# An attention and FFN layer on one core: mixing weights by eight indirect DMAs in place of one-hot matmuls

## What is computed

```python
def cond(x, weights, condition):          # weights [16, 32, 32]
    W = weights[condition]                # one 32x32 matrix for each batch
    return einsum('bct,bcd->bdt', x, W)   # mixes the 32 channels of a batch

x = x + attention(cond(x, cond_weights, tok), wq, wk, wv, wo)    # 32 heads, 8 kv heads, head size 128, rotary, causal
x = x + ffn(cond(x, cond2_weights, tok), qweight, scale, bias)   # fp8 quantized 512x512 linear layer
```

## Time and profile before

| | us |
|---|---|
| three executions | 573.87, 570.56, 572.55 |
| median | 572.55 |
| span of the profiled execution | 571.9 |
| TensorE busy in that span | 536.6 |
| VectorE, ScalarE, GpSimd busy | 423.0, 299.0, 278.4 |

### The profile page before, as it was taken

One profiled execution on the slowest core, in us unless ns is written; L12 is line 12 of the kernel. 1 busy time (PEld: TensorE's weight loads), 2 busy tenths in 40 slices (PEclk: granted clock), 3 DMA queues, 4 the chain that ended last, 5 costly groups with the idle time before them and its releaser, 6 DMA issues.

```text
span 571.9 us, 8828 instructions
## 1 busy us (share of the span) xinstructions
PE 536.6 (94%) x2987; PEld 432.6 (76%) x2988; DVE 423.0 (74%) x600; ACT 299.0 (52%) x504; POOL 278.4 (49%) x204
## 2 busy tenths in 40 slices
PE   4999999999999999999999999999999999899690
PEld 2987888888788878887888888878887888688420
DVE  5647366877697769776978697869777867776786
ACT  2503317563756475647564756475557555543724
POOL 6418314833684268327832774277427743720002
PEclk8899999999999999999999999999999999989866
DMA  7441300110111011101110220012002000000003
GB/s 250 161 148 43 123 2 1 42 52 1 47 55 66 0 56 51 58 0 65 53 47 0 73 68 24 0 73 84 7 0 73 6 0 1 0 2 1 1 0 147
DMA packets 18046, 26.87 MB, mean 47 GB/s; under 512 B 1995, under 2 KB 6219, under 8 KB 18028
## 3 DMA queue, kind: packets, MB, share of 16 engines
q1 hardware_dynamic: 18028, 26.63, 13.4%
HBM read 24.53 MB, written 2.10 MB: 47 GB/s over the span
## 4 chain that ended last, share of the span: by engine, by line
PE 67%; DVE 16%; issue 7%; ACT 7%; POOL 1%; DMA 1%; SPq 0%; DVEq 0%; ACTq 0%; POOLq 0%
PE bank L585 19%; PE bank L587 18%; PE bank L586 18%; PE bank L648 3%; PE bank L649 3%; PE bank L763 2%; DVE s_nat L855 2%; PE bank L633 2%; ACT p_st L433 1%; DVE s_nat L863 1%; PE bank L577 1%; DVE p_tr L868 1%; DVE s_sum L859 1%; DVE s_nat L849 1%; DVE s_nat L851 1%
## 5 line engine op out<-in xcount | busy, mean ns | idle before, releaser
L838 DVE TENSOR_TENSOR q_swap<-q_swap,cst 128x512 f32<-128x512 f32 x80 | 75.5, 944 | 68.5 <-ACT q_swap L404 68.4
L300 POOL TENSOR_TENSOR q_rot<-q_cos,q_swap 128x512 f32<-128x512 f32 x64 | 82.4, 1293 | 55.7 <-DVE q_cos L839 55.7
L585 PE MATMUL bank<-hT_hi,wq_hi 128*128 128x512 f32 x256 | 101.3, 396 | 4.4 <-DVE q_cos L839 4.4
L585 PE MATMUL bank<-wo_hi,o_hi 128*128 128x512 f32 x256 | 102.3, 400 | 0.4 <-issue 0.4
L587 PE MATMUL bank<-wo_hi,o_lo 128*128 128x512 f32 x256 | 100.9, 394 | 0.0
L586 PE MATMUL bank<-wo_lo,o_hi 128*128 128x512 f32 x256 | 100.5, 393 | 0.0
L587 PE MATMUL bank<-hT_hi,wq_lo 128*128 128x512 f32 x256 | 100.0, 391 | 0.0
L586 PE MATMUL bank<-hT_lo,wq_hi 128*128 128x512 f32 x256 | 100.0, 391 | 0.0
L403 ACT ACTIVATE q_swap<-bank 64x512 f32<-64x512 f32 x80 | 47.7, 596 | 63.1 <-POOL k_rot L300 24.6
L287 POOL TENSOR_TENSOR v_lo<-v_all,v_st 64x512 fp32r<-64x512 f32 x32 | 47.6, 1487 | 67.4 <-ACT v_st L414 64.6
L442 ACT ACTIVATE o_hi<-bank 128x512 fp32r<-128x512 f32 x64 | 38.1, 597 | 60.5 <-PE bank L649 60.1
(11 more groups left out here) (148 smaller groups left out, 947.9 us busy)
## 6 DMA issues: line engine op xcount, KB each, us to landing
raw_q<-in_L_attn_wq SPq DMA_DIRECT2D x8, 1024.0 KB, 5.5
raw_o<-in_L_attn_wo SPq DMA_DIRECT2D x8, 1024.0 KB, 5.3
xacc<-in_x SPq DMA_DIRECT2D x4, 512.0 KB, 8.4
raw_k<-in_L_attn_wk SPq DMA_DIRECT2D x8, 256.0 KB, 2.8
out<-xacc SPq DMA_DIRECT2D x8, 256.0 KB, 2.0
raw_o<-in_L_attn_wv SPq DMA_DIRECT2D x1, 1024.0 KB, 7.2
raw_q<-in_L_attn_wv SPq DMA_DIRECT2D x1, 1024.0 KB, 6.9
q_rot<-in_L_ffn_qweight SPq DMA_DIRECT2D x1, 1024.0 KB
```

Of the source, the lines that this page charges most:

```text
L300: pool.tensor_tensor(dst, q_cos[b][:], q_swap[b][:], ALU.add).then_inc(rope_done, 1)
L585: pe.matmul(dst, l_hi, r_hi, start=(i == 0), stop=False)
L838: dve.tensor_tensor(by_t(q_swap[b][:]), by_t(q_swap[b][:]), sin_b, ALU.mult)
```

## The change

Host code joins the two weight tables column by column into one array `conditions` of 16 x 32 = 512 rows with 64 numbers each. VectorE works out, for each partition and tile, the row number token x 32 + channel. GpSimd then issues eight indirect DMAs, one for each tile, which fetch 128 rows of 256 bytes into `picked`. `spread_blocks(i, w)` multiplies a pair of tiles with the block mask; both its operands are in SBUF. TensorE mixes a pair of tiles as soon as its blocks are there. The weight split, the selectors and the 96 selection matmuls go. SyncE issues the tokens, 8 columns of the constant table, x and wv, and then the rest of the table and the scale. GpSimd's four memsets move behind its low parts of wv, and ScalarE's identity copy behind its high parts. The clock-raising matmuls go from 14 to 24. The spreads for the FFN (w = 1) come after the last low half, ahead of the value copies.

```diff
         def _(sp):
             sp.dma_start(tok_i[:], itok.unsqueeze(0).broadcast_to([P, BATCH])).then_inc(dma_cond, 16)
-            sp.dma_start(wcond[:, :, 0:T], cond_v).then_inc(dma_cond, 16)
-            sp.dma_start(wcond[:, :, T:2 * T], cond2_v).then_inc(dma_cond, 16)
-            sp.dma_start(cst[:], consts).then_inc(dma_const, 16)
-            sp.dma_start(wsc[:], w_scale.broadcast_to([P, 1])).then_inc(dma_cond, 16)
+            sp.dma_start(cst[:, 0:C_FIRST], consts[:, 0:C_FIRST]).then_inc(dma_cond, 16)
             for t in range(0, TILES, 2):
                 ...
+            sp.dma_start(cst[:, C_FIRST:C_WIDTH], consts[:, C_FIRST:C_WIDTH]).then_inc(dma_const, 16)
+            sp.dma_start(wsc[:], w_scale.broadcast_to([P, 1])).then_inc(dma_const, 16)
         def _(pool):
-            pool.memset(p_st[0][:].bitcast(F32), 0.0)
-            pool.memset(v_lo[0][:].bitcast(F32), 0.0)
-            pool.memset(v_lo[1][:].bitcast(F32), 0.0)
-            pool.memset(p_st[1][:].bitcast(F32), 0.0).then_inc(const_done, 1)
+            pool.wait_ge(tok_step, 4)
+            for t in range(TILES):
+                pool.indirect_dma_start(out=picked[:, t, :], out_offset=None, in_=conds,
+                                        in_offset=bass.IndirectOffsetOnAxis(ap=tok_row[:, t:t + 1], axis=0)
+                                        ).then_inc(dma_pick[t // 2], 16)
...
-            pool.wait_ge(tok_step, 2)
-            for i in (1, 3):
-                select_pair(pool, i).then_inc(sel_lhs_pool, 1)
             for c in range(2 * KC):
                 ...
+            pool.memset(p_st[0][:].bitcast(F32), 0.0)
+            pool.memset(v_lo[0][:].bitcast(F32), 0.0)
+            pool.memset(v_lo[1][:].bitcast(F32), 0.0)
+            pool.memset(p_st[1][:].bitcast(F32), 0.0).then_inc(const_done, 1)
         def _(act):
-            act.wait_ge(dma_cond, 64)
-            act.activation(wc_part[0], wcond, ACT.Copy).then_inc(wc_step, 1)
-            for i in (1, 2):
-                act.wait_ge(wc_step, 2 * i)
-                act.activation(wc_part[i], wc_rest, ACT.Copy).then_inc(wc_step, 1)
-            act.wait_ge(dma_const, 16)
-            act.activation(ident_bf[:], ident, ACT.Copy).then_inc(const_done, 1)
...
             for c in range(KC, 2 * KC):
                 wv_high(c)
+            act.wait_ge(dma_const, 32)
+            act.activation(ident_bf[:], ident, ACT.Copy).then_inc(const_done, 1)
             pe.wait_ge(warm_done, 1)
-            raise_clock(14)
+            raise_clock(24)
             for t in range(TILES):
-                pe.wait_ge(sel_lhs_pool if t // 2 % 2 else sel_lhs, t // 4 + 1)
-                for i in range(3):
-                    ...
-            for t in range(TILES):
-                pe.wait_ge(wbd_done, 1 if t < TPU else 3)
+                pe.wait_ge(wbd_done, t // 2 + 1)
                 pe.wait_ge(dma_x[t // 2], 16)
                 if t >= 3:
                     pe.wait_ge(h_lo_done, t - 2)
-            dve.wait_ge(dma_cond, 64)
-            dve.wait_ge(dma_const, 16)
+            dve.wait_ge(dma_cond, 32)
             dve.tensor_copy(tok_f[:], tok_i[:]).then_inc(tok_step, 1)
             dve.wait_ge(tok_step, 1)
...
+            dve.tensor_tensor(tok_own[:], tok_f[:].rearrange("p (t b) -> p t b", b=BPT), own_b, ALU.mult).then_inc(tok_step, 1)
             dve.wait_ge(tok_step, 2)
...
+            dve.tensor_reduce(tok_sum[:], tok_own[:], AX_X, ALU.add).then_inc(tok_step, 1)
+            dve.wait_ge(tok_step, 3)
+            dve.tensor_scalar(tok_row[:], tok_sum[:], float(T), cst[:, C_CHAN:C_CHAN + 1], ALU.mult,
+                              ALU.add).then_inc(tok_step, 1)
+            def spread_blocks(i, w):
+                src = picked[:, 2 * i:2 * i + 2, w * T:(w + 1) * T].unsqueeze(2).broadcast_to([P, 2, BPT, T])
+                dst = wbd1[i // 2][:, 2 * (i % 2):2 * (i % 2) + 2] if w == 0 else wbd2[:, 2 * i:2 * i + 2]
+                dve.wait_ge(dma_pick[i], 32)
+                return dve.tensor_tensor(dst, src, block_b, ALU.mult)
...
-            for t in range(TILES):
+            for i in range(TILES // 2):
+                spread_blocks(i, 0).then_inc(wbd_done, 1)
+                if i >= 2:
+                    h_low(2 * i - 4)
+                    h_low(2 * i - 3)
+            for t in range(TPU, TILES):
                 h_low(t)
+            for i in range(TILES // 2):
+                spread_blocks(i, 1)
+            dve.wait_ge(dma_const, 32)
```

More of the change, by code:

```diff
@@ L35 @@
 LEAST = 1.5 * 2.0 ** 14
-C_COS, C_SIN, C_SVAL, C_CSEL, C_BLOCK, C_IDENT, C_TRI, C_ONE = 0, 32, 64, 68, 100, 104, 232, 264
+C_BLOCK, C_CHAN, C_COS, C_SIN, C_IDENT, C_TRI, C_ONE = 0, 4, 8, 40, 72, 200, 232
+C_FIRST = C_COS
 C_WIDTH = C_ONE + P
@@ L64, in constant_table @@
     table[:, C_SIN:C_SIN + T] = np.sin(emb).T * sign[:, None]
-    table[:, C_SVAL:C_SVAL + 4] = (P // T) * np.arange(4)[None, :] + part[:, None] // T
-    table[:, C_CSEL:C_CSEL + T] = part[:, None] % T == np.arange(T)[None, :]
+    table[:, C_CHAN] = part % T
     table[:, C_BLOCK:C_BLOCK + 4] = part[:, None] // T == np.arange(4)[None, :]
@@ L72, in constant_table, with build @@
     return table
-def build(nc, x, itok, cond_w, wq, wk, wv, wo, cond2_w, qweight, w_scale, bias, consts, out):
+def build(nc, x, itok, conds, wq, wk, wv, wo, qweight, w_scale, bias, consts, out):
     with ExitStack() as ctx:
@@ L120, in build @@
         tok_f = sb("tok_f", [P, BATCH])
-        tok_eq = sb("tok_eq", [P, 4, BATCH])
+        tok_own = sb("tok_own", [P, TILES, BPT])
+        tok_sum = sb("tok_sum", [P, TILES])
+        tok_row = sb("tok_row", [P, TILES], I32)
+        picked = sb("picked", [P, TILES, 2 * T])
         w8 = sb("w8", [P, KC, HID], BF16)
@@ L135, in build @@
         w_ps = bank[6:8]
-        sel_ps = [s_ps, o_ps[0]]
         dma_const, dma_x, dma_cond, dma_wv, dma_ffn = (sem(n) for n in ("dma_const", "dma_x0", "dma_cond", "dma_wv", "dma_ffn"))
+        dma_pick = [sem(f"dma_pick{i}") for i in range(TILES // 2)]
         dma_x = [dma_x] + [sem(f"dma_x{i}") for i in range(1, TILES // 2)]
@@ L173, in build @@
         mask_b = cst[:, C_TRI:C_TRI + T].unsqueeze(1).broadcast_to([P, TPU * REP, T])
-        csel_b = cst[:, C_CSEL:C_CSEL + T].unsqueeze(1).unsqueeze(1).broadcast_to([P, 4, 2 * BPT, T])
-        block_b = cst[:, C_BLOCK:C_BLOCK + BPT].unsqueeze(1).unsqueeze(3).broadcast_to([P, TPU, BPT, T])
+        own_b = cst[:, C_BLOCK:C_BLOCK + BPT].unsqueeze(1).broadcast_to([P, TILES, BPT])
+        block_b = cst[:, C_BLOCK:C_BLOCK + BPT].unsqueeze(1).unsqueeze(3).broadcast_to([P, 2, BPT, T])
         flat = lambda a: a[:].rearrange("p a t -> p (a t)")
[L180 to L184, removed]
         warm = w8[:, 0, :]
         wbd1 = [a[:].rearrange("p (t b d) -> p t b d", t=TPU, b=BPT) for a in q_swap]
-        wcond = k_rot[:, 0:4 * 2 * T].rearrange("p (k n) -> p k n", k=4)
         wT = [a[:].bitcast(BF16).rearrange("p (c o) -> p c o", c=KC // 2) for a in q_cos]
@@ L775, in _ @@
             dve.memset(ones_r[BIAS_ROWS - 1:BIAS_ROWS, :].bitcast(F32), 1.0)
-            dve.wait_ge(dma_cond, 64)
-            dve.wait_ge(dma_const, 16)
+            dve.wait_ge(dma_cond, 32)
             dve.tensor_copy(tok_f[:], tok_i[:]).then_inc(tok_step, 1)
             dve.wait_ge(tok_step, 1)
[L781 to L786, removed]
-            dve.wait_ge(tok_step, 2)
[L788 to L795, removed]
-                    dve.tensor_tensor(dst, picked[:, :, w, :].unsqueeze(2).broadcast_to([P, TPU, BPT, T]), block_b,
-                                      ALU.mult).then_inc(wbd_done, 1)
+            dve.tensor_tensor(tok_own[:], tok_f[:].rearrange("p (t b) -> p t b", b=BPT), own_b, ALU.mult).then_inc(tok_step, 1)
+            dve.wait_ge(tok_step, 2)
+            dve.tensor_reduce(tok_sum[:], tok_own[:], AX_X, ALU.add).then_inc(tok_step, 1)
[7 more added lines that the diff above has]
+                return dve.tensor_tensor(dst, src, block_b, ALU.mult)
             def h_low(t):
@@ L1066, in _ @@
             add_back(7)
-_INS = ["x", "itok_B_0_15", "L0_cond_weights", "L0_attn_wq", "L0_attn_wk", "L0_attn_wv", "L0_attn_wo",
-        "L0_cond2_weights", "L0_ffn_qweight", "L0_ffn_weight_scale", "L0_ffn_bias"]
+_INS = ["x", "itok_B_0_15", "conditions", "L0_attn_wq", "L0_attn_wk", "L0_attn_wv", "L0_attn_wo",
+        "L0_ffn_qweight", "L0_ffn_weight_scale", "L0_ffn_bias"]
 def kernel(**inputs):
@@ L1078 @@
     arrays, args = {}, []
+    both = np.concatenate([inputs["L0_cond_weights"], inputs["L0_cond2_weights"]], axis=2)
+    inputs["conditions"] = both.reshape(CONDS * T, 2 * T)
     for name in _INS:
```

8 lines of the change are left out of this document (1 added, 7 removed).

## The result

The changed kernel takes 576.89 us (median of four, 575.74 to 578.57), the kernel before 571.55 (four, 569.96 to 573.87). The ratio is 1.0107, 95% interval 1.0063 to 1.0150: slower, and by more than the noise. The forecast was no change at 572.8; the measured time lies in its range, in the case that had 0.21.

What follows compares the result with a forecast made beforehand. From the first mixing matmul the kernel was taken as one TensorE stream: V 3.0 us earlier less a 3.2 us stall makes 0.2 later, span 571.9 + 0.2 = 572.1, as a median 572.8 us; range 567.0 to 578.0.

Steps and rivals of the forecast that it cites:

- the case that had 0.21: Whole kernel: slower than before; 0.19 for slow gathers plus 0.02 for a clock loss over 2.9 us with a slower gather.
- V: Start of the first value matmul, at 24.79 us in the kernel before; forecast at 21.8, 3.0 us earlier.
- Tokens: Head: constant columns landed at 3.9 us, four small VectorE steps 0.9, hand-over to GpSimd 0.1; gathers start at 4.9 us.
- Gathers, holding GpSimd: Head: each indirect DMA holds GpSimd 1.1 us, eight take 8.8, to 13.7 us.
- Gathers, landing: Head: 2.7 us from issue to landing, bounds 2.3 to 9.2; pairs land at 9.8, 12.0, 14.2 and 16.4 us.
- Mixing: Head: first spreads wait for single GpSimd passes; spread 3 at 18.25, low half 2 at 18.95, then tiles 5 to 7.
- The clock: Head: TensorE's idle stretches of 2.1, 2.6, 1.1 and 3.2 us, all under 4.3, leave the granted clock up.
- the rival with 0.11: Head: the clock falls, 4.7 us of dense work run at 1.2 GHz and lose half: 575.2 us; chance 0.11.
- The second spreads: Before the first value copy: four spreads take turns with GpSimd's passes, 1.6 us apart, so TensorE stalls 3.2 us.
- The rival that they cost nothing: Second spreads slip in between GpSimd's passes without a stall, V's 3.0 us stay: 569.6 us; chance 0.13.
- At nothing: Head: x, value weights, GpSimd's memsets, ScalarE's identity copy and ten more clock matmuls cost nothing; everything later moves with the stage.
- slow gathers: Head: 2.05 us a gather holds GpSimd 7.6 us more, V near 29.4, with the stall 7.8: 580.3 us; chance 0.19.

Runs made afterwards that it cites:

- the kernels with free ports: The changed kernel with GpSimd's first value-weight pass held until all first spreads are done (573.54 us, one run), or with those low parts on VectorE (574.68 us, 1.0051).
- The held loads: Low parts of the first value weights on VectorE, plus SyncE's next three loads held until the last gathers landed, against the changed kernel; 572.62 us, ratio to before 1.0042.
- the kernels with held loads and without them: With: low parts on VectorE and SyncE's three later loads held, 572.62 us. Without: all four edits less that hold, 570.90 us, ratio 1.0000.
- all four edits: Changed kernel with low parts on VectorE, SyncE's three later loads held, FFN spreads behind value copies 8 to 11, 40 clock matmuls; 566.55 us, ratio to before 0.9940.
- the one with held loads alone: The changed kernel with nothing but SyncE's three later loads held until the last gathers have landed; one run, 572.46 us.
- the kernel with 24 clock matmuls: The kernel with all four edits, but 24 clock matmuls instead of 40; 569.29 us, ratio to before 0.9988.

## Why the prediction was right or wrong

**The forecast of no change did not come true, and the range held by luck.** It holds 576.89 because it was stretched for gathers of up to 2.05 us, which did not happen. V was forecast at 21.8 and came at 27.9; the stall, forecast at 3.2, came at 2.4 and made up for 0.8 of that. By the steps:

*Tokens.* 4.9 us; the first gather starts at 5.32. Right but for 0.4.

*Gathers, holding GpSimd: nearly right.* 1.1 us was forecast; measured 0.95 of work, but 1.25 from start to start. The last ends at 15.2 instead of 13.7. This is 1.5 us and well inside the bounds; the case of gathers of 2.05 us did not happen.

*Gathers, landing: the term that was mis-sized most.* I took 2.7 us, the constant table's, and it was 5.9 to 6.9 from issue. The bounds (2.3 to 9.2) held it. The table had landed before SyncE's traffic ran at full rate, the x transfers within it, and the gathers fly within it too: x's row was the nearer one. The last pair landed at about 20.5 (the spread of the kernels with free ports: 20.54, 20.57) instead of 16.4: of these 4.1 us 1.5 are the gathers', 2.6 the landing's. The held loads show 2.5 us, about what I had taken, when nothing else moves. The Trainium skill (DMA: Bandwidth & Descriptors, Queues, rings and completion order) has the DMA engines take turns between queues, and I let that speak for a short landing. No run here shows the turns; what the runs show is that beside 390 GB/s the landing was 6 us and not short.

*Mixing: the collision was named and its kind was wrong.* I had VectorE wait for one pass at most. At the second spreads that was right. Spread 1, however, was passed over by all of the four passes in a row, 4.73 us. It put the last spread at 22.02 where its landing allowed 20.5. Yet the last spread, on which my sum ran, wasn't what set V: TensorE mixed the last six tiles from 20.62 on without a wait, so V was set by the end of spread 1 and by the clock. The kernel with the low parts on VectorE shows the price of the two together: V 3.5 us earlier.

*The clock.* I counted idle stretches of 2.1, 2.6, 1.1 and 3.2 us and judged them safe because a stretch of 4.3 had been the only one to cool it. The first stretch became 5.1 (8.13 to 13.22) as the first landing came 3 us late, and the clock fell 2.9 us after the last matmul. From 20.62 to 24.6 the mixing then ran at 1.2 GHz, which costs half of that, 2.0 us. (The row that I read for the return has it at about 17.9, 5.1 us after 12.77 and not 4.7.) Also the yardstick failed: stretches of 2.2 and 2.4 us were enough twice (the kernels with held loads and without them), and not in the other cases. So the rival with 0.11 did happen, on top of the landing, and for the reason that I had set aside.

Together: with its passes on VectorE the kernel has V at 24.4, set by the last landing, 2.6 us after the 21.8 forecast. Six tiles from 20.62 on at full clock would have put V at 25.9 (27.90 less the 2.0 above), so the passes at spread 1 add 1.5, and the clock 2.0 more. That is the 6.1 us. The 25.9 is an estimate from rows; no run has the passes beside spread 1 and a clock that stays up.

*The second spreads: right.* The stall was forecast at 3.2 and measured at 2.4, with spreads of 1.48 to 1.54 us taking turns with passes of 1.3 to 1.5. Moving them away took it out. The rival that they cost nothing falls. The sentence on V without these collisions doesn't come out of the prediction's own steps: the last landing at 16.4, 0.35, 0.7 and 2.8 give 20.25, 4.5 us before the kernel before and not 3.9.

*At nothing.* x, the value weights, the memsets and the identity copy cost nothing, as said; TensorE never waited for wo_lo in the changed kernel. The trunk passed on what the head lost or gained: -3.9 us in V became -3.4 in time, and 54.2 us lie between V and the first transpose mark both in the kernel before and in the one with all four edits.

Of the rivals, "slow gathers" had the right side, but its 7.8 us are for gathers of 2.05 us. Only its last sentence, on the landing, names what happened.

## What to carry to other kernels

A small DMA that the critical path waits for should be priced by transfers that flew beside the same traffic, not by ones that landed before it began; if larger loads behind it aren't due yet, hold them until it has landed (4.1 us of V and 3.4 us of time here). Where an engine's products and GpSimd's passes read SBUF together, count every pass that is ready, not one, and give such passes to an engine that is idle at that time. An edit that replaces work on TensorE by a wait must be priced with the clock: the same matmuls cost twice as much after it (two tiles in 3.78 us against 1.95).

## What the runs showed of the hardware

An indirect DMA of 128 rows of 256 bytes holds GpSimd for 0.95 us (the first 1.10, one beside VectorE's two-operand products 1.17 to 1.30), 1.25 with the issue, and lands 2.3 to 2.5 us after its issue when nothing else moves and 5.6 to 7.7 beside loads at 390 GB/s.

VectorE's access to SBUF beside a stream of GpSimd passes has two forms. Where it asked at the start of a stream it took turns (1.5 us each for 0.42 of work). Where it asked in the middle, it waited for the whole of what was left of it (spread 1 in four kernels, and spread 3 in the one with held loads alone). What decides between them stays open.

TensorE's granted clock fell 2.9 to 5.2 us after the last matmul ahead of a wait, at times when work had resumed (at 13.4 in the kernel with 24 clock matmuls, 0.4 us after mixing began), and waits of 2.2 and 2.4 us brought it down in two kernels while others of 2.4 did not. It came back 3.5 to 6.0 us after work had begun again, and the first piece of the changed kernel's mixing, 3.78 us, did not bring it back.
